# A 64-state scan layer on one core: sums over states tiled and put later, preparation put later, carry copies on GpSimd, and five of 32 even inputs made by ScalarE

## What is computed

```
u      = layernorm(x @ W_in[:, :C]) * gamma + beta
dt, B, C = split(u @ W_dt + b_dt)              # 8, 64 and 64 columns
delta  = softplus(dt @ W_dtr + b_dtr)
h_n[l] = exp(delta[l] * A_n) * h_n[l-1] + delta[l] * u[l] * B_n[l]      # 64 states n, 128 channels
y[l]   = sum over n of h_n[l] * C_n[l]  +  u[l] * D
out    = x + (y + xc * silu(xc)) @ W_out       # xc: a 3x3 depthwise convolution of a projection of x
```

## Time and profile before

| | us |
|---|---|
| median of three runs | 10412.63 |
| the profiled execution | 10406.57 |
| its span in the trace | 10404.1 |
| from the first scan of the layer (2838.3) to the end of its last (5937.3 + 2.3) | 3101.3 |
| TensorE, VectorE, ScalarE, GpSimd busy, share of the whole span | 93%, 81%, 77%, 57% |
| granted TensorE clock, mean over the span | 0.973 |

### The profile page before, as it was taken

The page is one execution under the profiler, slowest core; times in us unless marked ns, Lnnn a source line. Parts: engine busy times, 40 slices in busy tenths (PEclk is TensorE's granted clock), DMA queues, the critical chain, the costliest instruction groups (busy, mean ns, idle before and its releaser), DMA issues. The chain is left out here.

```text
span 10404.1 us, 137498 instructions
## 1 busy us (share of the span) xinstructions
PE 9674.0 (93%) x45956; PEld 5155.6 (50%) x45956; DVE 8382.7 (81%) x8102; ACT 7988.8 (77%) x14637; POOL 5928.8 (57%) x2628
## 2 busy tenths in 40 slices
PE   9999999999899999999999999998999998888885
PEld 6767767677544444444444444443333333333332
DVE  7858858678499999999999911119999999999997
ACT  5646646556488888888888655559999999999996
POOL 0000000000188888888888600009999999999996
PEclk9999999999899999999999999999999999999997
DMA  0000000000045555555555400015656566666666
GB/s 38 0 1 0 0 1 0 0 0 0 24 174 173 177 175 173 175 175 174 175 176 174 148 8 8 8 38 189 196 194 199 191 196 194 201 195 201 195 199 225
DMA packets 335956, 1240.78 MB, mean 119 GB/s; under 512 B 38768, under 2 KB 38896, under 8 KB 331888
## 3 DMA queue, kind: packets, MB, share of 16 engines
q1 hardware_dynamic: 335472, 1234.73, 35.6%
HBM read 1144.40 MB, written 56.62 MB: 115 GB/s over the span
## 5 line engine op out<-in xcount | busy, mean ns | idle before, releaser
L951 POOL TENSOR_TENSOR l_hc<-l_h,l_hc 128x1024 f32<-128x1024 f32 x1024 | 2397.4, 2364 | 452.9 <-DVE l_h L1049 452.4
L1863 POOL TENSOR_TENSOR l_ring<-l_ring 128x1024 f32<-128x1024 f32 x1024 | 2453.8, 2426 | 152.6 <-DVE l_ring L1941 151.7
L1941 DVE TENSOR_TENSOR_SCAN l_ring<-l_ring,l_carry,l_ps 128x1024 f32<-128x1024 f32 x960 | 2199.3, 2332 | 1.0
L688 PE MATMUL l_ps<-l_hc,w_sb 128*128 128x512 f32 x4096 | 1936.4, 595 | 68.6 <-POOL l_hc L951 61.2
L1049 DVE TENSOR_TENSOR_SCAN l_h<-l_decay,l_carry,l_ps 128x1024 f32<-128x1024 f32 x768 | 1760.0, 2333 | 4.3 <-issue 0.4
L116 POOL COPY l_qm<-l_q 128x128 f32 x128 | 82.3, 645 | 2576.3 <-PE l_ps L188 2180.6
L829 ACT ACTIVATE l_decay<-l_delta,w_sb 128x1024 f32<-128x1024 f32 x1024 | 1152.9, 1138 | 168.3 <-DVE l_h L1049 168.0
L1753 ACT ACTIVATE l_xt<-l_duT,l_BT 128x128 f32<-128x128 f32 x4096 | 1247.2, 390 | 0.0
L842 ACT ACTIVATE l_xt<-l_duT,l_BT 128x128 f32<-128x128 f32 x4096 | 1246.0, 388 | 0.0
L1545 PE MATMUL l_ps<-l_ring,w_sb 64*64 64x512 f32 x8192 | 1189.0, 653 | 2.2 <-ACT l_gate L1679 1.4
L212 PE MATMUL l_ps<-l_attnT,l_vT 128*128 128x128 f32 x8192 | 1096.2, 277 | 1.3 <-ACT l_attnT L283 1.3
(11 more groups left out here) (238 smaller groups left out, 14808.8 us busy)
## 6 DMA issues: line engine op xcount, KB each, us to landing
l_hc<-l_rows_dram SPq DMA_DIRECT2D x1024, 512.0 KB, 3.7
l_ring<-l_rows_dram SPq DMA_DIRECT2D x1024, 512.0 KB, 5.1
l_crossed<-l_delta SPq DMA_DIRECT2D x128, 256.0 KB, 3.5
l_gate_dram<-l_gate SPq DMA_DIRECT2D x32, 512.0 KB, 6.6
l_recon_dram<-l_recon SPq DMA_DIRECT2D x32, 512.0 KB, 6.5
l_gate<-l_gate_dram SPq DMA_DIRECT2D x32, 512.0 KB, 5.6
l_xw<-x_dram SPq DMA_DIRECT2D x30, 513.5 KB, 7.1
x_dram<-x SPq DMA_DIRECT2D x16, 512.0 KB, 2.6
```

The source lines that it names most:

```text
L688: ins = nc.tensor.matmul(y_sum[:, half(j)], ident, hc[:, unit % CS, half(j)], start=q == 0, stop=q == S1 - 1)
L951: nc.gpsimd.tensor_tensor(hc[:, unit % CS, :], h[:, unit % HS, :], hc[:, unit % CS, :], ALU.mult).then_inc(hc_done, 1)
L1863: nc.gpsimd.tensor_tensor(hc[:, unit % CS, :], h[:, unit % HS, :], hc[:, unit % CS, :], ALU.mult).then_inc(hc_done, 1)
L1941: nc.vector.tensor_tensor_scan(h[:, unit % HS, order], decay[:, unit % DS, order], x_now[:, order], before, ALU.mult, ALU.add).then_inc(sc ...
```

## The change

1. Sums. `add_pair` takes the place of `add_state`. A pair's two products are added together by matmuls of a 64x64 quarter of the identity, in two phases of four matmuls; the odd unit's lower half is added to the upper half of `y_sum` and the other way round. It runs two pairs behind (`P - 2`) where `add_state` ran one behind. `y_sum` is read at k = 1, not 0.
2. For that the odd units have their channels' halves swapped: their decays read `crossed`, a copy of `delta` with halves exchanged, made by two DMAs a chunk on SyncE's queue (`cross_delta`, between the loads of units 62 and 63, after the last decay of the chunk); `duT_copy` swaps the halves of `duT`; `A` is rolled by 64 for odd units.
3. The turned pairs. In pairs k = 6, 13, 20, 24, 29 (`TURNED`) the even unit's input comes from ScalarE and TensorE too (`turned_input(P, 0)`, `turn_back(P, 0)`), and VectorE's `even_input` is not run. `BT` has 37 columns, not 32.
4. Keeps. The copy into `carry` goes from VectorE to GpSimd, ahead of each product.
5. Preparation is put two or three k later on every engine; `store_rows` from unit 26 to 30. `duT`'s transposes, `silu` and the residual stay where they were. `CS` is 7, not 5. `part` lies in `z2`, with two more waits (`low_ready`, `stack_ready`).

```diff
+TURNED = (6, 13, 20, 24, 29)
+BTW = SEL + len(TURNED)
...
-    HS, DS, CS, XS = 4, 4, 5, 4
+    HS, DS, CS, XS = 4, 4, 7, 4
...
+            def cross_delta(K):
+                sp.wait_ge(delta_ready, K + 1)
+                at_least(sp, decay_ready, S1 * K)
+                for side in range(2):
+                    sp.dma_start(crossed[64 * side:64 * side + 64, :],
+                                 delta[64 - 64 * side:128 - 64 * side, K % 2, :]).then_inc(crossed_in, 16)
...
-                    if q == 26 and K + 1 < NCH:
+                    if q == 30 and K + 1 < NCH:
                         store_rows(K + 1)
+                    if q == 62 and K + 1 < NCH:
+                        cross_delta(K + 1)
...
-            def add_state(unit):
+            def add_pair(P, phase):
+                K, k = divmod(P, PAIRS)
+                if phase == 0:
+                    if k == 0:
+                        at_least(pe, y_out, K)
+                    pe.wait_ge(hc_done, 2 * P + 2)
+                    at_least(pe, sum_mm, 2 * P)
+                else:
+                    pe.wait_ge(first_half_mm, P + 1)
+                lower, upper = slice(0, 64), slice(64, 128)
+                for own, other, j in ((lower, upper, phase), (upper, lower, 1 - phase)):
+                    for odd, to in enumerate((own, other)):
+                        ins = nc.tensor.matmul(ps[to, 4 + j, :], ident[own, own], hc[own, (2 * P + odd) % CS, half(j)],
+                                               start=k == 0 and phase == 0, stop=k == PAIRS - 1 and phase == 1)
...
                     P = K * PAIRS + k
-                    turn_back(P)
-                    if P:
-                        add_state(2 * P - 2)
+                    turn_back(P, 1)
                     if k in CONV:
                         convolution(K, *CONV[k])
...
-                        if k in (14, 15):
-                            prep_delta(K + 1, k - 14)
+                        if k in (16, 17):
+                            prep_delta(K + 1, k - 16)
...
-                    if P + 1 < NCH * PAIRS:
+                    if P > 1:
+                        add_pair(P - 2, 0)
+                    if k + 1 in TURNED:
+                        turn_back(P + 1, 0)
+                    elif P + 1 < NCH * PAIRS:
                         broadcast_B(P + 1, p if k + 1 < PAIRS else 1 - p)
-                    if P:
-                        add_state(2 * P - 1)
+                    if P > 1:
+                        add_pair(P - 2, 1)
...
+                if q == 1:
+                    act.wait_ge(crossed_in, 32 * K + 32)
                 at_least(act, scan_done, unit - DS + 1)
-                nc.scalar.activation(decay[:, unit % DS, :], delta[:, p, :], ACT.Exp,
+                nc.scalar.activation(decay[:, unit % DS, :], crossed[:] if q % 2 else delta[:, p, :], ACT.Exp,
...
                         own = p if k + 1 < PAIRS else 1 - p
+                        if k + 1 in TURNED:
+                            turned_input(P + 1, 0, own)
                         decays(2 * P + 2, own)
-                        odd_input(P + 1, own)
+                        turned_input(P + 1, 1, own)
                         decays(2 * P + 3, own)
...
-                        if k == 16:
+                        if k == 18:
                             soft_exp(K + 1, 1 - p)
-                        if k == 17:
+                        if k == 19:
                             soft_log(K + 1)
...
             def product(unit):
+                K, q = divmod(unit, S1)
+                pool.wait_ge(scan_done, unit + 1)
+                if K % NC < NC - 1:
+                    nc.gpsimd.tensor_copy(carry[:, q:q + 1], h[:, unit % HS, CH - 1:CH]).then_inc(kept, 1)
                 pool.wait_ge(c_in[unit % CS], 16 * (unit // CS) + 16)
-                pool.wait_ge(scan_done, unit + 1)
...
-                        if k == 12:
+                        if k == 14:
                             split_rest(K + 1)
...
-                        if k == 18:
+                        if k == 20:
                             soft_low(K + 1)
...
-                        if k == 21:
+                        if k == 23:
                             input_rate(K + 1, 1 - p)
...
-                    if k == 0 and K:
+                    if k == 1 and K:
                         add_y(K - 1, 1 - p)
-                    if P + 1 < NCH * PAIRS:
+                    if P + 1 < NCH * PAIRS and k + 1 not in TURNED:
                         even_input(P + 1, p if k + 1 < PAIRS else 1 - p)
-                    if K % NC < NC - 1:
-                        keep(2 * P)
-                        keep(2 * P + 1)
...
-                        if k == 4:
+                        if k == 7:
                             rstds(K + 1)
                             newton(K + 1)
```

More of the change, by code:

```diff
@@ L534, in keeps_before, with turned_before, halves_before @@
             return 2 * (b * (NC - 1) * PAIRS + min(c, NC - 1) * PAIRS + (k if c < NC - 1 else 0))
+        def turned_before(P):
+            return P // PAIRS * len(TURNED) + sum(k < P % PAIRS for k in TURNED)
+        def halves_before(P, odd):
+            return 2 * (P + turned_before(P)) + (2 if odd and P % PAIRS in TURNED else 0)
         block = ctx.enter_context(nc.Block())
@@ L670, in broadcast_B, with turn_back @@
                 ins.then_inc(b_mm, 1)
-            def turn_back(P):
-                at_least(pe, scan_done, 2 * P)
+            def turn_back(P, odd):
+                n = halves_before(P, odd)
+                at_least(pe, scan_done, 2 * P + odd - 1)
                 for hf in range(2):
-                    pe.wait_ge(xt_ready, 2 * P + hf + 1)
+                    pe.wait_ge(xt_ready, n + hf + 1)
                     for t in range(4):
-                        ins = nc.tensor.transpose(odd_bank(hf)[:, t * 128:(t + 1) * 128],
-                                                  xt[:, (2 * P + hf) % XS, t * 128:(t + 1) * 128], ident)
+                        ins = nc.tensor.transpose(state_bank(odd, hf)[:, t * 128:(t + 1) * 128],
+                                                  xt[:, (n + hf) % XS, t * 128:(t + 1) * 128], ident)
                     ins.then_inc(xt_mm, 1)
-            def add_state(unit):
[L683 to L690, removed]
+            def add_pair(P, phase):
[12 more added lines that the diff above has]
+                                               start=k == 0 and phase == 0, stop=k == PAIRS - 1 and phase == 1)
+                if phase == 1:
+                    ins.then_inc(sum_mm, 2)
+                else:
+                    ins.then_inc(first_half_mm, 1)
             pe.wait_ge(weights_in, 32)
@@ L776, in split_high @@
                 act.wait_ge(bdt_out, 2 * K + 2)
-                nc.scalar.activation(part[:], rest[0:PARTS * SEL, :], ACT.Identity,
+                at_least(act, low_ready, 2 * K)
+                nc.scalar.activation(part, rest[0:PARTS * SEL, :], ACT.Identity,
                                      scale=w[0:PARTS * SEL, L1_AT["below_top"]][:, 0:1]).then_inc(part_ready, 1)
@@ L837, in odd_input @@
                     act.wait_ge(bt_ready, K + 1)
+                n = halves_before(P, odd)
+                at = k if odd else SEL + TURNED.index(k)
                 for hf in range(2):
-                    at_least(act, xt_mm, 2 * P + hf - XS + 1)
+                    at_least(act, xt_mm, n + hf - XS + 1)
                     for t in range(4):
                         blk = 4 * hf + t
-                        ins = nc.scalar.activation(xt[:, (2 * P + hf) % XS, t * 128:(t + 1) * 128], duT[:, p, blk, :],
-                                                   ACT.Identity, scale=BT[:, p, blk, k:k + 1])
+                        own = duT[:, p, blk, :].rearrange("p (s d) -> p s d", s=2)
+                        into = xt[:, (n + hf) % XS, t * 128:(t + 1) * 128].rearrange("p (s d) -> p s d", s=2)
+                        ins = nc.scalar.activation(into, own if odd else own[:, ::-1, :], ACT.Identity,
+                                                   scale=BT[:, p, blk, at:at + 1])
                     ins.then_inc(xt_ready, 1)
@@ L1040, in scan @@
                 K, q = divmod(unit, S1)
-                if odd:
-                    dve.wait_ge(xt_mm, 2 * P + 2)
-                else:
-                    dve.wait_ge(inp_done, P + 1)
+                if odd or P % PAIRS in TURNED:
+                    dve.wait_ge(xt_mm, halves_before(P, odd) + 2)
+                else:
+                    dve.wait_ge(inp_done, P + 1 - turned_before(P))
+                if not odd:
                     at_least(dve, kept, keeps_before(P - 1) if P else 0)
@@ L2138, in layer1_arrays @@
     by_unit = _np.arange(S1).reshape(2, S1 // 2).T.reshape(-1)
-    even_B, odd_B, all_C = slice(R1, R1 + SEL), slice(R1 + SEL, R1 + S1), R1 + S1 + by_unit
+    even_B, all_C = slice(R1, R1 + SEL), R1 + S1 + by_unit
+    turned_B = [*range(R1 + SEL, R1 + S1), *(R1 + k for k in TURNED)]
```

100 lines of the change are left out of this document (51 added, 49 removed).

## The result

10340.47 us, the median of four runs (10337.94 to 10343.11), against 10410.69 (10406.84 to 10412.78): ratio 0.9933, interval 0.9921 to 0.9945, 70 us faster. Forecast: 10345. The profiled execution's span is 10336.1 us.

The account below looks back on a forecast made before the run. VectorE was taken as the bound (98%), TensorE close behind. The terms -97 + 0 + 0 - 31 + 0 + 60 = -68 on 10406.6 gave 10338.6, with 6 us for the median 10345; range 10250 to 10430 us.

Parts of the forecast that it names:

- rival A: The forecast: VectorE gains 128 us, gives half back to ScalarE in k = 20 to 22; 10345 us, chance 0.47.
- (a): Turned pairs: 80 even inputs leave VectorE, a turned pair's period falls from 5.74 to 4.53; -97 us.
- (b): Keeps leave VectorE: 768 copies, hidden while the scan waits for the even input; 0, ends 0 and -79 us.
- (c): The 768 keep copies on GpSimd: 0.2 to 0.3 us each, its chunk 184 us, under VectorE's need; 0.
- rival C: Slower: at 0.54 us a copy the keeps make GpSimd the bound; 10507 us, chance 0.16.
- no stall: GpSimd at k = 20 to 23: lags of 4 to 6 us where 6.8 is allowed, so no scan waits.
- (d): Tiled, late sums on TensorE: VectorE's 41 us of waits go, 10 come back at add_y; -31 us.
- (e): Loads and crossing on SyncE's queue: rows and crossed copy land in time or off the path; 0.
- (f): ScalarE gains 80 inputs, late at k = 20 to 22: VectorE waits 4.0 us in 15 chunks; +60 us.
- B: Rival: ScalarE keeps up and VectorE's own time alone sets the end; 10285 us, chance 0.26.
- the prediction's own sign: Forecast wrong if VectorE's waits for ScalarE sum to under 20 or over 120 us.

Follow-up runs that it names:

- root_psum: The kernel with the change, but ScalarE writes the 8 columns of root into PSUM, not SBUF; 10309.7 us.
- no_turned: The kernel with the change, but with no turned pairs (TURNED empty), all other parts kept; 10368.5 us.
- without_20: The kernel with the change, but pair 20 of a chunk is not turned any more; 10299.4 us.
- at_8_not_20: The kernel with the change, but pair 8 is turned in the place of pair 20; 10300.3 us.
- six_root_gate: The kernel with the change, but pairs 6, 8, 10, 13, 24, 29 turned, root in PSUM, gate_conv(K, 0) at k = 22; 10247.5 us, ratio 0.9845 against the kernel before.

## Why the prediction was right, and where only its sum was

The forecast was 68 us, the layer gave 70.1. The main mechanism, rival A, is shown; but two errors cancel, so the closeness of the sum is in part luck.

- **(a)** Turned pairs: 80 even inputs fewer, period 4.50. Right; 1.24 a pair, 99 us for 97.
- **(b)** Keeps free on VectorE: right in the ordinary pairs. I named what hides them, the even input, and didn't see that (a) removes that cover in five pairs of each chunk. Left on VectorE they would have cost 18 us there.
- **(c)** GpSimd's copy: 190 ns each, and 0.14 us from its start to the next product's (3263.27 to 3263.41), for my 0.25; the 0.14 that I had estimated beside it was the better figure. GpSimd didn't become the bound (rival C, 0.16, is out): 456 of 500. But "no stall" was wrong. I followed its lateness only at k = 20 to 23 and against the scans, not at k = 4 to 7, and not for an operation that has no semaphore with GpSimd at all. That is the step that failed: VectorE's own operations are not independent of a busy GpSimd. Its price is 28.8 us (root_psum) where it was 7.5 before: +21.
- **(d)** Tiled, late sums: -31 forecast. no_turned, which has them, is 40.4 us under before in the layer, with the moves of (b), (c) and the preparation in it, and with some of the wait at k = 7. So undersized by 10 or more. The waits that I had named, 25 for broadcasts and 16 of `add_y`, are 7.6 and 4.9 in no_turned, 29 us less; where the other 11 come from stays open, since the tiled sums, the later preparation and the keeps were not taken apart. `add_y` waits once, at the end of the layer; of my 10 nothing came back in the chunks between.
- **(e)** Loads and crossing: right. GpSimd waits 4.4 us for rows in all; ScalarE 24.6 for the crossed copy, off the path.
- **(f)** ScalarE's lead: 7.0, 1.8, 0 forecast, 7.3, 2.1, 0.2 found. The stall: 4.0 a chunk forecast, 3.7 by without_20. The gate waits 2.0 a chunk, not 2.8, the odd scan 0.9 for its decay or its transposes, not 1.2, and 0.8 is a wait for a broadcast that I didn't have.

Sum of the measured: -40.4 - 99 + 55 + 11 (the part of k = 7 that comes with the turned pairs: 9.67 for 8.72, in 11 chunks) = -73, for the layer's -70.1. B was out by the prediction's own sign: VectorE's waits for ScalarE at k = 21 are 40.6 us (30.0 at the gate, 10.6 at scans), between 20 and 120.

## What to carry to other kernels

When work moves to an engine with time to spare, follow that engine's lead step by step through its densest stretch, not its share of busy time: moving the same turned pair from k = 20 to k = 8 turned a loss into a gain, once k = 7 was free. A saving in front of a wait is worth nothing until the wait is gone, and what hides a small operation must be looked for again after every edit. In this kernel VectorE's small operations with all their inputs in SBUF were cheap only while GpSimd was idle; one operand in PSUM made them so under a busy GpSimd too, and the next operation, left in SBUF, took over part of the wait.

## What the runs showed of the hardware that I had not expected

A VectorE operation on 8 columns with two SBUF inputs, 0.17 us by itself, lasts until GpSimd's running 1024-column product ends: 2.35 us at the median in the change, and up to 2.95 in at_8_not_20, where the next product began before the operation got through. One with a single SBUF input lasts up to 2.58 us (L1043 in six_root_gate). Scans and even inputs, which read one operand from PSUM, were not longer for GpSimd's fuller list (2.33 and 1.21 us, as before).

And TensorE's clock. In the layer before, the granted clock is 1.00; in the layer of the change it is 0.96. The two stretches, of before and of the change:

```profile
2838.00:5937.00 3099.00, 2965.73 (x10918) 1526.00 (x10919) 3043.42 (x2499) 2623.89 (x5543) 2651.48 (x1142) 1.00 0.51 174
```

```profile
2838.00:5867.20 3029.20, 2514.65 (x15470) 1026.23 (x15474) 2940.73 (x1652) 2802.65 (x6184) 2745.03 (x1910) 0.96 0.55 182
```

One place is at k = 21. There ScalarE's lateness let TensorE stand still for 2.15 and 0.45 us around 3341; this is what followed, by engine in a stretch of 2 us (0.50 is the clock), and TensorE in order of time:

```profile
3342.90:3344.90 2.00, 2.00 (x6) 0.30 (x8) 1.91 (x1) 2.00 (x6) 2.00 (x3) 0.50 0.13 53
```

```profile
3340.84 0.63 PE L698 MATMUL l_ps<-w_sb,l_xt 128*128 128x128 f32 x4 [2.15 <-ACT l_xt L882]
3341.91 0.66 PE L698 MATMUL l_ps<-w_sb,l_xt 128*128 128x128 f32 x4 [0.45 <-ACT l_xt L882]
3342.41 1.68 PE L679 MATMUL l_ps<-l_yg,w_sb 128*128 128x512 f32 x2
3344.02 1.99 PE L715 MATMUL l_ps<-l_hc,w_sb 64*64 64x512 f32 x8
...
3346.51 1.09 PE L715 MATMUL l_ps<-l_hc,w_sb 64*64 64x512 f32 x8
```

The granted clock was 0.50, the 1.2 GHz level, and a phase of sums took 1.99 us where it takes 1.09. The broadcast behind it came late, and that is VectorE's wait of 1.28: in that period a late ScalarE was paid for three times, at the decay, at the broadcast and at the gate. Each of the 15 chunks that prepare another has such a stretch of low clock at k = 21 or 22; without_20 has it in four of them. Both have others at k = 7 and 8 and at k = 0 to 2 (0.69 in the mean from 3266 to 3270 in the change), and VectorE's waits for broadcasts just behind those, at k = 3 and 8, are 6.5 us in all. My sum has no term for the clock, and what it costs in all was not tried.
